# Joining the two narrow causal blocks of each attention half into one unit, moving row maxima one unit earlier, and reordering small steps at the stage seams

## The reference

```python
x = x + 0.5 * ffn(layernorm(x), gate_w, base_w, base_b, lora_A, lora_B)
x = x + attn(layernorm(x), Wq, Wk, Wv, Wo)
x = x + 0.5 * ffn(layernorm(x), gate_w, base_w, base_b, lora_A, lora_B)

# ffn: a dense layer, and two of eight low-rank experts per token
top, selected = top_k(x @ gate_w.T, 2);  w = softmax(top)
ffn = x @ base_w.T + base_b + 2.0 * sum_e w[e] * (x @ lora_A[e].T) @ lora_B[e].T

# attn: 32 query heads in 8 groups of 4 that share a key/value head, head size 32, rotary positions
att = softmax(causal(q @ k.T / sqrt(32)))
attn = (att @ v) @ Wo
```

## Time and profile before

| | |
|---|---|
| median of 3 runs | 1575.81 us (1573.46 to 1577.57) |
| profiled execution, its own time | 1575.4 us |
| its span | 1573.6 us |
| granted TensorE clock, mean over the span | 0.983 |
| PE busy | 1524.4 us (97%) |
| DVE busy | 967.3 us (61%) |
| POOL busy | 694.0 us (44%) |
| ACT busy | 587.0 us (37%) |

### The profile page before, as it was taken

How to read it: one execution, slowest core, us unless ns; L and a number is a source line. 1 busy time by engine, 2 the same in 40 slices (tenths; PEclk the granted TensorE clock), 3 DMA queues, 4 the chain that set the end, 5 groups by cost and what they waited for, 6 DMA issues and landing times. The chain is left out here.

```text
span 1573.6 us, 26210 instructions
## 1 busy us (share of the span) xinstructions
PE 1524.4 (97%) x9184; PEld 1191.0 (76%) x9184; DVE 967.3 (61%) x2727; ACT 587.0 (37%) x1185; POOL 694.0 (44%) x414
## 2 busy tenths in 40 slices
PE   7999998999999969999999999999999999999999
PEld 7999998888888845555555555555478999999998
DVE  7545464556473468888888888888655434343433
ACT  4333233211111125666666666666633222121210
POOL 1222222533343415888888888888612101010100
PEclk8999999999999969999999999999999999999999
DMA  6322324342322362344433333441161212121201
GB/s 230 124 109 98 123 96 149 134 135 82 120 94 81 111 133 62 82 98 101 90 81 76 75 82 83 100 103 30 48 224 59 67 55 68 53 73 47 79 16 41
DMA packets 118774, 145.96 MB, mean 93 GB/s; under 512 B 40976, under 2 KB 77072, under 8 KB 118384
## 3 DMA queue, kind: packets, MB, share of 16 engines
q1 hardware_dynamic: 90064, 120.59, 26.5%
q10 hardware_dynamic: 28592, 23.86, 4.6%
HBM read 95.66 MB, written 53.51 MB: 95 GB/s over the span
## 5 line engine op out<-in xcount | busy, mean ns | idle before, releaser
L1504 ACT ACTIVATE at_probs<-ps 128x512 f32<-128x512 f32 (+3 forms) x768 | 324.6, 494 | 151.2 <-PE ps L1413 149.1
L1573 DVE CUSTOM_DVE_ANT_0 ps<-ps,at_score_mask 128x512 f32<-128x512 f32 (+3 forms) x512 | 290.7, 618 | 36.4 <-PE ps L1402 33.4
L329 POOL TENSOR_TENSOR f_x_ring<-f_x_ring,f_half_bias 128x1024 f32<-128x1024 f32 x32 | 77.3, 2416 | 312.8 <-DVE f_h L590 312.3
L1342 POOL TENSOR_TENSOR at_added<-at_added,at_probs 128x2048 f32<-128x2048 f32 (+1 forms) x60 | 211.4, 3523 | 2.1
L1413 PE MATMUL ps<-at_qs,at_ks 98*128 98x512 f32 (+3 forms) x528 | 192.3, 390 | 4.3 <-ACT at_probs L1504 2.9
L1402 PE MATMUL ps<-at_ks,at_qs 96*128 96x512 f32 (+3 forms) x528 | 175.4, 368 | 12.0 <-DMA at_ks<-scr_k_hi 11.3
L1413 PEld LDWEIGHTS ps<-at_qs,at_ks 98*128 98x128 f32 x528 | 97.3, 193 | 110.5 <-ACT at_probs L1504 86.4
L1428 PE MATMUL ps<-at_probs,at_vs 128*32 128x512 f32 (+3 forms) x1536 | 162.8, 496 | 0.0
L1573 DVE CUSTOM_DVE_ANT_0 ps<-ps,at_score_mask,at_part_max 128x128 f32<-128x128 f32 (+3 forms) x256 | 133.2, 556 | 12.8 <-issue 10.4
L48 PE MATMUL f_ps<-f_wt_hi,f_hT_hi 128*128 128x400 f32 (+1 forms) x384 | 134.3, 350 | 3.2 <-DVE f_hT_lo L594 3.2
L48 PE MATMUL ps<-f_wt_hi,f_hT_hi 128*128 128x400 f32 (+1 forms) x384 | 132.1, 344 | 0.0
(11 more groups left out here) (164 smaller groups left out, 3163.4 us busy)
## 6 DMA issues: line engine op xcount, KB each, us to landing
at_qs<-scr_q_hi SPq DMA_DIRECT2D x20, 512.0 KB, 5.9
f_x_ring<-in_L_attn_resid SPq DMA_DIRECT2D x16, 512.0 KB, 3.5
x<-f_x_ring SPq DMA_DIRECT2D x16, 512.0 KB, 2.7
early<-x SPq DMA_DIRECT2D x16, 512.0 KB, 3.3
scr_q_hi<-qkv_rope_hi ACTq DMA_DIRECT2D x32, 256.0 KB, 2.0
scr_q_lo<-qkv_rope_lo ACTq DMA_DIRECT2D x32, 256.0 KB, 2.3
scr_ctx<-at_ctxn SPq DMA_DIRECT2D x32, 256.0 KB, 2.3
shared<-scr_ctx SPq DMA_DIRECT2D x16, 512.0 KB, 4.5
```

The source lines that it names most:

```text
L329: pool.tensor_tensor(x_ring[:, u, :], x_ring[:, u, :], half_bias[:], ALU.add).then_inc(bias_added, 1)
L1342: pool.tensor_tensor(added[:, heads, :], first, probs[:, u % PROBS, heads, :], ALU.add).then_inc(added_done, 1)
L1504: act.activation(probs[:, u % PROBS, g, 0:z - a], score_ps[(u * G + g) % BANKS][:, 0:z - a], ACT.Exp, scale=SCALE).then_inc(exp_done, 1)
L1573: dve.tensor_tensor_reduce(out=src, in0=src, in1=mask, scale=1.0, scalar=part_max[:, g, own] if c else -3.0e38, op0=ALU.add, op1=ALU.max, ...
```

## The change

**Units.** Key blocks 2 and 3 of the first half, and 6 and 7 of the second, become one unit each: 256 + 128 columns, side by side in one PSUM bank and one place of `probs`. A group has 10 units (`NU = 10`), its last of half 0 is now unit 2. PE's products are the same in number and size; ACT has one exponential of 384 columns where it had one of 256 and one of 128 (40 a group for 48); POOL has one mask of 4 by 2 by 128 for two of 4 by 128 (6 masks a group for 8). `ADDED` is now `range(3, 8)`, the same five blocks. `probs` is a ring over `(NU * n + u) % PROBS`.

**Row maxima.** The items for group m begin in the last unit of group m - 2 and end in the last but one of group m - 1, and `TURN_B` comes a unit earlier. SP's `store(n - 1, 0)` moves behind `load_rows(n, 1)` of the next group.

**Seams.** The identity is loaded from ACT's queue, so SP begins with `x`. In FFN1 POOL adds the bias to tiles 0 and 1 once `low_s` of that tile is made, and both before it begins with Wq. In FFN2 it waits for `hT_lo_done` 2. In QKV the loads of tiles 4 and 5 come after the fourth of the eight Wk/Wv pieces. The output projection of each half waits for the slot of that half's sum alone.

The core of the diff (the same index changes are left out where they repeat):

```diff
-            if prep:
-                sp.dma_start(ident[:], consts["identity"]).then_inc(ident_loaded, 16)
             load_x(sp, 0, 0)
...
+            def add_bias(i, u):
+                pool.wait_ge(h_ready, 4 * i + u + 1)
+                pool.tensor_tensor(x_ring[:, u, :], x_ring[:, u, :], half_bias[:], ALU.add).then_inc(bias_added, 1)
...
             if attn:
-                pool.wait_ge(w_lo_done, KC + 1)
+                pool.wait_ge(hT_lo_done, 2)
...
+            if prep:
+                pool.wait_ge(low_ready, 1)
+            add_bias(0, 0)
+            if prep:
+                pool.wait_ge(low_ready, 2)
+            add_bias(0, 1)
+            for u in range(4):
+                if u >= 2:
+                    add_bias(0, u)
+                if prep:
+                    low_wq(0, u)
...
+            if prep:
+                act.dma_start(ident[:], consts["identity"]).then_inc(ident_loaded, 16)
...
+                if j == WRAW:
+                    sp.wait_ge(h_turned, TC + 1)
+                    for slot in range(2):
+                        load_x(TC + slot, slot)
...
-            sp.wait_ge(h_turned, TC + 1)
-            with sp.Fori(TC // 2, NT // 2, 1) as i:
+            with sp.Fori(TC // 2 + 1, NT // 2, 1) as i:
...
-    ADDED = range(4, 9)
-    ADDS_TO = {4: 1, 5: 1, 6: 2, 7: 3, 8: 5}
+    ADDED = range(3, 8)
+    ADDS_TO = {3: 1, 4: 1, 5: 2, 6: 3, 7: 5}
...
-        units = [(half, j) for half in range(2) for j in range(QH * (half + 1))]
+
+        units = [(0, (0,)), (0, (1,)), (0, (2, 3))] + [(1, (j,)) for j in range(NQ - 2)] + [(1, (NQ - 2, NQ - 1))]
         NU = len(units)
-        LAST = {QH - 1: 0, NU - 1: 1}
-        LAST_OF = (QH - 1, NU - 1)
+        H0 = QH - 1
+        LAST = {H0 - 1: 0, NU - 1: 1}
+        LAST_OF = (H0 - 1, NU - 1)
...
+        def blocks(u):
+
+            half, js = units[u]
+            out, at = [], 0
+            for j in js:
+                a = max(j * P - half * HALF, 0)
+                out.append((j, slice(a, HALF), slice(at, at + HALF - a)))
+                at += HALF - a
+            return out
...
+        for m in range(2, NG + 1):
+            windows = [(m - 2, NU - 1)] + [(m - 1, u) for u in range(NU - 1)]
+            for at, items in zip(windows, spread(first, weight, [room[u] for _, u in windows])):
+                placed[at] = of(m, items) if m < NG else []
+            lead = placed[m - 2, NU - 1]
+            assert len(lead) >= SLOTS or m == NG
+            lead.insert(min(SLOTS, len(lead)), (m - 1, TURN_B))
+        placed[NG - 1, NU - 1] = []
...
             for n in range(NG):
                 load_rows(n, 1)
+                if n:
+                    store(n - 1, 0)
...
-                tile = probs[:, u % PROBS, :, 0:P]
+                count = len(units[u][1])
+                tile = probs[:, (NU * n + u) % PROBS, :, :].rearrange("p g (b n) -> p g b n", b=2)[:, :, 0:count, 0:P]
...
-                                   pattern=[[0, G], [1, P]], channel_multiplier=-1).then_inc(mask_done, 1)
+                                   pattern=[[0, G], [0, count], [1, P]], channel_multiplier=-1).then_inc(mask_done, 1)
...
+                for j, at, cols in blocks(u):
+                    last = pe.matmul(score_ps[x % BANKS][:, cols], ks[:, nm, j * P:(j + 1) * P], qs[nm][0:KROWS + 2, half, g, at],
+                                     start=True, stop=True)
+                last.then_inc(scores_done, 1)
...
-                if half:
-                    pe.wait_ge(slot_read, len(number) + SLOTS)
+                pe.wait_ge(slot_read, number[NG - 1, ("sum", half)] + (SLOTS + 1))
```

More of the change, by code:

```diff
@@ L1173, in attention_stage @@
         weight = [row_keys(it[1], it[3]) + 800 if it[0] == "row" else 900 for it in first]
-        room = [queries(u)[1] - queries(u)[0] + 1200 for u in range(NU)]
+        room = [width(u) + 1200 for u in range(NU)]
         def spread(items, weights, spaces):
@@ L1202, in attention_stage @@
         early = rows[OPEN + 8:OPEN + 20]
-        for u in range(QH):
-            placed[0, u] = of(0, early[3 * u:3 * u + 3])
-        for u, items in enumerate(spread([TURN_A] + rows[at_a:], weight[at_a:], room[QH:])):
-            placed[0, QH + u] = of(1, items)
-        for n in range(1, NG):
-            for u, items in enumerate(spread(first, weight, room)):
-                placed[n, u] = of(n + 1, items) if n + 1 < NG else []
-            placed[n, 0].insert(min(SLOTS - 1, len(placed[n, 0])), (n, TURN_B))
+        for u in range(H0):
+            placed[0, u] = of(0, early[4 * u:4 * u + 4])
+        for u, items in enumerate(spread([TURN_A] + rows[at_a:], weight[at_a:], room[H0:NU - 1])):
+            placed[0, H0 + u] = of(1, items)
+        for m in range(2, NG + 1):
[6 more added lines that the diff above has]
+        placed[NG - 1, NU - 1] = []
         for n in range(NG):
@@ L1218, in attention_stage @@
             for u in range(NU):
-                if n == 0 and u in (0, QH):
-                    for key in BEFORE[u // QH] + [key for part in BETWEEN[u // QH] for key in part]:
+                if n == 0 and u in (0, H0):
+                    for key in BEFORE[u // H0] + [key for part in BETWEEN[u // H0] for key in part]:
                         number[key] = len(number)
@@ L1306, in _ @@
                     store(n - 1, 1)
-                store(n, 0)
+            store(NG - 1, 0)
             store(NG - 1, 1)
@@ L1341, in add @@
                     first = added[:, heads, :]
-                pool.tensor_tensor(added[:, heads, :], first, probs[:, u % PROBS, heads, :], ALU.add).then_inc(added_done, 1)
+                pool.tensor_tensor(added[:, heads, :], first, probs[:, (NU * n + u) % PROBS, heads, :], ALU.add).then_inc(added_done, 1)
             def join(n):
@@ L1447, in sums @@
                 for u in APART[half]:
-                    a, z = queries(u)
-                    for g in range(G):
-                        last = pe.matmul(out[g * DH:(g + 1) * DH, a - half * HALF:z - half * HALF], ones[:],
-                                         probs[:, u % PROBS, g, 0:z - a], start=u == 0, stop=u in LAST)
+                    for j, at, cols in blocks(u):
+                        for g in range(G):
+                            last = pe.matmul(out[g * DH:(g + 1) * DH, at], ones[:], probs[:, (NU * n + u) % PROBS, g, cols],
+                                             start=u == 0, stop=u in LAST and j == units[u][1][-1])
                 last.then_inc(slot_filled, 1)
@@ L1456, in _ @@
                 for u in range(NU):
-                    if n == 0 and u in (0, QH):
-                        half = u // QH
+                    if n == 0 and u in (0, H0):
+                        half = u // H0
                         for m, it in BEFORE[half]:
@@ L1471, in _ @@
                         for m, it in items:
-                            slot_item(m, it, n == NG - 1)
+                            slot_item(m, it, (m, it) == (NG - 1, TURN_B))
                     if u in LAST:
@@ L1598, in add_last @@
                     first = added[:]
-                dve.tensor_tensor(added[:], first, probs[:, u % PROBS, :, :], ALU.add).then_inc(last_added, 1)
+                dve.tensor_tensor(added[:], first, probs[:, (NU * (NG - 1) + u) % PROBS, :, :], ALU.add).then_inc(last_added, 1)
             def low_ctx(t):
@@ L1607, in _ @@
                 for u in range(NU):
-                    if n == 0 and u in (0, QH):
-                        for m, it in BEFORE[u // QH]:
+                    if n == 0 and u in (0, H0):
+                        for m, it in BEFORE[u // H0]:
                             slot_item(m, it)
-                        for items in BETWEEN[u // QH]:
+                        for items in BETWEEN[u // H0]:
                             for m, it in items:
```

106 lines of the change are left out of this document (51 added, 55 removed).

## The result

| | before | changed | ratio |
|---|---|---|---|
| median, first measurement (4 runs each) | 1575.34 us | 1563.34 us (1560.88 to 1565.67) | 0.9923 (0.9906 to 0.994) |
| median, a later measurement (15 and 4 runs) | 1578.90 us | 1562.48 us (1560.89 to 1564.17) | 0.9902 (0.9887 to 0.9917) |
| span of the profiled execution | 1573.6 us | 1563.9 us | |

The change makes the kernel faster by 12 us in the first measurement and by 16 in the second. The forecast was 1554.4, a gain of 21 us; the result lies inside the range of 1547 to 1564, by 0.7 us.

A forecast was written before the change was run, and what follows sets the result against it. Attention was taken as bound by PE, with POOL close behind. Attention 9.0, FFN1 3.4, QKV 4.4, FFN2 4.4 and start 0.2 sum to 21.4 us off 1575.4; with 0.4 for the median, 1554.4, range 1547 to 1564.

The forecast's parts named there:

- Joined units: Attention: two units fewer a group save switches between scores and products, 0.8 us a group on PE alone.
- Groups 1 to 14: Attention's steady groups: likeliest gain 0.5 us each, 7.0 us in all (2.8 to 11.2).
- the moved rows: Attention: row items a unit earlier cost nothing, since DVE has 99 us idle in 560; otherwise PE waits.
- POOL's chain: Attention, second half: POOL's masks and adds end late, so PE waits and 0.3 of the 0.8 us comes back.
- Rival 3: Attention: joining gives nothing, as a dear double mask makes POOL late by the whole 0.8 us; 1561.4 us, 14%.
- rival 4: Attention: kernel slower because the four-level double mask runs slowly, over about 2.9 us; 1592 us at 3.2; 3%.
- First and last group: Attention: 0.3 us in group 0, 1.3 in the last, plus 0.4 from the wait behind it.
- FFN1: First FFN: DVE's stand-still beside POOL's bias addition, PE's gaps and the half clock go; 3.4 us (1.5 to 4.5).
- Rival 2: Both FFN stages: POOL's additions only collide with DVE's next routing instead; about 1559.5 us, 20%.
- QKV: QKV stage: earlier load of tile 4 removes PE's gap of 2.87 and the half clock; 4.4 us (2.9 to 4.6).
- FFN2: Second FFN: later bias halving removes the stand-still, gap of 2.70 and half clock; 4.4 us (2.7 to 4.4).
- Start: Kernel start: the x load goes out 0.45 us earlier, worth 0.2 us (0 to 2).

The follow-up runs named there:

- before_light: Kernel before, 12 units, row maxima over half of each item's columns and POOL's later additions over 128 of 512: 34.66 us between sums.
- both_light: Changed kernel, row maxima over half of each item's columns and POOL's later additions over 128 of 512: 33.77 us between sums, 1542.92 us in all.
- ahead12: Kernel before, 12 units, only the row items and TURN_B moved a unit earlier: 35.37 us between sums, 1583.37 us in all.
- dve_light: Changed kernel, row maxima read only half of each row item's columns: 34.39 us between sums, 1551.86 us in all.
- place2: Changed kernel, row items dealt differently to the ten places, DVE's first-half reciprocal one unit earlier: 33.88 us between sums, 1549.38 us, ratio 0.9813.
- seams2: Changed kernel, identity back on SP, ACT's second Wq high part later, its square root for tile 4 earlier: 1560.57 us, ratio 0.9882.
- attn_only: Kernel before with only the change's attention stage, other stages kept: 1573.17 us, ratio 0.9968.
- place1: Changed kernel, only the numbers of row items in the ten places differ: 34.22 us between sums, 1553.18 us, ratio 0.9836.
- rows_own: Changed kernel, row items, TURN_B and SP's store placed as before the change: 37.91 us between sums, 1614.53 us, ratio 1.023.

## Why the prediction was right and wrong

**The total.** The sign was right and the range held, but with 0.7 us to spare in the first measurement, and with a third of the forecast gain (7.0 of 21.4) not there at all. The stages sum to a gain of 9.7 us by one trace and 14.6 by the other. That the total came out inside is owed to the width of the range and to the seams, so in part to luck.

**Joined units: the price was about right, the bound wrong.** The 0.8 us a group on PE was 0.89 or somewhat more (`before_light` against `both_light`). The double mask, taken as 1.28, took 1.10.

**Groups 1 to 14, 7.0 us forecast, 0 measured: the failed step is the moved rows, "Costed at nothing".** It rested on DVE's 99 idle microseconds in 560, an average over the group. In the changed kernel's trace the idle time lies around the sums (DVE busy 1.30 of 3 us from 764, 1.13 of 2 from 779, 1.41 of 3 from 798); from 781 to 798 DVE is full. The move put the last row items of a group beside others and left the rest of the deal to a table of PE's room (`width + 1200`) that knows nothing of DVE's. `ahead12` prices the move at 0.6 us a group without joining, `dve_light` finds 0.4 of it with joined units before POOL holds, and `place2` gives back 0.9 by another deal. The prediction had named this ("PE waits ahead of a row item", "for a row slot at the new places") and given it no size.

**POOL's chain, 0.3 us forecast, hidden.** `dve_light` shows it as the next bound, 34.39 against the forecast 34.27. The chain from the mask to the end of the last addition, taken as 11.72, took 11.68 in the changed kernel. The reasoning was sound, but it spoke of the second limit. Rival 3 had nearly the time (1561.4) with the wrong cause, a dear mask. In rival 4 the threshold of about 2.9 us doesn't follow from its own two waits, which give 2.8; at 1.10 it is out of play.

**First and last group.** 1.1 (0.3 forecast) and 1.8 (1.7 forecast, the 0.4 behind it included: the gap ahead of the projection fell from 0.92 to 0.43).

**FFN1, 3.4 forecast.** Rival 2, the moved collision, came true here. In the eight traces with this code QKV starts at 262.77 to 267.19, mean 264.2, against 265.54 to 266.44, mean 266.05, in the four with the code of before: 1.8 us of gain on average with the start, with single traces from 1.1 us of loss to 3.3 of gain; that is nearer to the 2.0 that the Trainium skill's rule of the port lock gave ("SBUF — State Buffer", Who interferes with whom) than to 3.4. The trace agrees with the rule where two inputs are concerned: in `seams2` L635 ends at 55.87, POOL's addition at 55.85.

**QKV, 4.4 forecast, 3.0 and 3.2 in the traces of the changed kernel.** The gap of 2.87 shrank to 1.31: the tile's path goes through ACT's queue too, which the step hadn't followed. But the trace of before was a lucky one: in the other three with the old code of this stage (`attn_only`, `before_light`, `ahead12`) the gap was 4.0 to 4.2. Over all traces the stage took 298.0 on average (4) and 293.3 (8), a gain of 4.7. The size was right. ACT's place in the path was not seen; the gap that it leaves is 0 to 1.4 us from run to run.

**FFN2, 4.4 forecast, 4.8 measured.** Right: the stand-still and the fall of the clock behind it both went.

**Start, 0.2 forecast.** The earlier x was worth nothing that can be seen; the identity, issued at 0.79 as before, reached PE at 4.8 to 5.4 us in the eight traces, where it had been 2.6 to 2.7.

## What to carry to other kernels

Before work is moved from one place of a repeating schedule to another, add up the helper engine's work place by place, against the time of each place: an engine at 81% on average can be the bound for half of the cycle. When a saving doesn't come, cut one helper's work at a time, then both, and do the same in the kernel before: the three or four distances are the stack of bounds. They hold for that one schedule: another deal moved POOL's from 34.4 to 33.9. And an operation that is moved clear of one collision stays clear only if it waits for the end of what it collided with in every tile; here the change did so for the first two tiles, and the third was hit.

## What the runs showed of the hardware

A mask over 128x1024 took 1.10 us beside 0.63 to 0.65 for 128x512: a fixed part of 2 x 0.64 - 1.10, about 0.2, an estimate. A cast on DVE over two columns, with one input in SBUF, stood still as well beside POOL's addition, 2.33 us in `place2` (0.17 in `seams2`), so not only operations with two inputs are held up:

```profile
51.43 2.40 POOL L321 TENSOR_TENSOR f_x_ring<-f_x_ring,f_half_bias 128x1024 f32<-128x1024 f32 x1
51.52 0.20 ACT L496 ACTIVATE f_expgap<-f_gap 128x1 f32<-128x1 f32 x1 [1.41 <-DVE f_gap L621]
51.52 2.33 DVE L623 CAST f_idx_f<-f_top_idx 128x2 f32<-128x2 uint32 x1
```

The same gap doesn't always bring the clock down. At the start of FFN2 `attn_only` has a gap of 2.70 us and `ahead12` one of 2.72; the four microseconds behind it (from, to, length, PE busy, clock) read, in this order:

```profile
1191.70:1195.70 4.00, 3.93 (x14) 0.58 0.00 0
```
```profile
1203.80:1207.80 4.00, 3.91 (x22) 1.00 0.00 0
```

From the first product of the output projection to the end it is 427.3 us in the one and 426.1 in the other, so the low clock costs about 1.2 us there (1.7 in the prediction), an estimate from two traces, and it is a term that comes or goes from run to run. In FFN1 a gap of 3.48 us left the clock at full as well (`place1`), and one of 2.65 did (`before_light`), while one of 2.05 in the kernel before was followed by the low clock. Gaps of 1.1 to 1.8 us left it at full in the FFN and QKV stages of every trace, but not in the groups of `rows_own`, where it fell behind 11 of 13 gaps of 1.3 to 1.65 us.
